# Moving each batch's norm two attention slots ahead, with temporary tiles of its own for rope

## The chip, the cores and the metric

The kernel runs on one core of one Trainium2 chip. The metric is the device time in microseconds of that core. Each time is the median of several executions.

## The reference

Four layers follow one another on an activation `x` of 4 batches, 512 positions and 512 channels, all in fp32. Only the first two matter for this change.

```python
# layer 0: modulated LayerNorm, attention with 16 heads of 32, latent keys and values, residual
h = (x - mean(x)) * rsqrt(var(x) + 1e-5) * (1 + scale) + shift
q = h @ Wq.T ; c_kv = h @ Wkd.T ; k = c_kv @ Wku.T ; v = c_kv @ Wvu.T
q, k = rope(q), rope(k)                          # z * cos + rotate_half(z) * sin
x = x + softmax(mask(q k.T / sqrt(32))) v @ Wo.T # the mask hides later blocks of 128

# layer 1: modulated RMSNorm, attention with 8 query heads of 64 and one key head, residual, gated MLP
h = x * rsqrt(mean(x * x) + 1e-6) * w * (1 + scale)
q, k = rope(h @ Wq.T), rope(h @ Wk.T) ; v = h @ Wv.T
x = x + softmax(q k.T / sqrt(64)) v @ Wo.T
x = x + (silu(h2 @ Wg.T) * (h2 @ Wu.T)) @ Wd.T
```

Layer 2 is another attention and MLP, layer 3 is a set of experts with an output projection.

## The kernel before

Activations are kept channel by position: `x` lies in SBUF as 128 partitions, 4 channel tiles, 4 batches, 512 positions. Every engine runs its own instruction stream; each engine has one semaphore that counts its finished steps, and a step waits until the count of another engine has come far enough. An instruction that waits holds everything behind it on its engine.

The attentions and all that surrounds them in layers 0 and 1 are one woven step, `layers01`. `weave` writes the order of all engines by hand. The attention of one batch of one layer is a **slot**; there are eight, `heads0` of batches 0 to 3 and then `heads1` of batches 0 to 3. A slot is a row of **quads**, four units (128 queries of one head) each: 16 quads in a slot of `heads0`, 8 in one of `heads1`. For each quad TensorE (PE) multiplies the scores (line 675), VectorE (DVE) takes the maximum (L740 with the mask, L744 without), ScalarE (ACT) the exponential (L765), PE turns the probabilities (L682), ACT and DVE copy them (L770, L747) in turns, PE multiplies by the values (L695) and spreads the reciprocal of the sums (L704), and DVE divides (L755). A unit's keys are 128 to 512 wide in layer 0, and 512 in layer 1.

A quad has four **points** at which other work, the **side** work of the slot, is inserted into every engine's stream. The side work is a list of beats; `weave` spreads the list of a slot evenly over its points. Its parts are

- the norm of a batch (`SideNorm`). For layer 0 it has seven beats: POOL sums the four tiles of x (L351, L358), an empty beat, PE takes the mean (L342) with DVE's subtraction (L394) and ACT's squares (L371), POOL sums the squares (L354, L358), an empty beat, PE takes the variance (L342) with ACT's logarithm and exponential (L376, L379, a table load before each), and last DVE scales (L406) and ACT shifts (L382). For layer 1 it has five beats, without the mean, the subtraction and the shift. The result goes to the tile `hN`, the sums to `t1`.
- the projections (`SideLinear`, L441): ten groups in layer 0, of which five read `hN` with four 512 wide products each; six groups in layer 1, all of which read `hN`.
- rope (`SideRope`): eight or five tiles. PE permutes (L474), DVE multiplies by sine into `hN[:, g % 2]` (L482), POOL multiplies by cosine (L490) and adds (L494).
- the output projection of an attention and its residual (`post`, L441 and L1314), four beats.

Before, the side work of slot m is: the norm of batch m+1 (counted over both layers), its projections, and then the output projection of slot m-1 and the rope of m+1 in turns. The norm, projection and rope of the first batch stand ahead of slot 0. In slot 0 the norm's seven beats lie in quads 0 to 4 and the first projection in quad 4; in slots 1 and 2 the norm's lie in quads 0 to 3 and the first projection follows at quad 4. In slots 3 to 6 the layer-1 norm is in quads 0 to 3 (slot 3) and 0 to 1 (slots 4 to 6), and the first projection in quad 4 and quad 2. All side matmuls inside the slots share one PSUM bank, 7, so each waits until the one before it has been read. Scores use banks 0 to 3.

Since rope writes into `hN`, the norm of the next batch waits for the last rope addition of this one (`h_free`).

SyncE (SP) issues loads in its own order. Once the last rope addition of layer 0 is done it refills the cosine and sine tables with eight transfers, and behind them it loads layer 1's query weights into the place of layer 0's (`l_wq1`), which groups 1 to 4 of `proj1` wait for. Group 0 of `proj1` uses other weights, that were loaded at the start.

Of the kernel before, what the change touches and what calls it, by code (L numbers as in the profile page):

```python
# [266 lines left out]
class Woven(Step):  # L267

    def __init__(s, seq):
# [7 lines left out]
    def waiter(s, k, e, at):  # L279
        past = dict.fromkeys(NAMES, 0)  # L280

        def after(name, b, kind, index):
            who, n = s.i[(name, b, kind, index)]
            if n > past[who]:
                past[who] = n
                e.wait_ge(k.done[who], at[who] + n)
        return after

    def pe(s, k, e, b, at):
        start_wait(k, e, at, "act", "dve", "pool")  # L290
        after = s.waiter(k, e, at)
# [3 lines left out]
    def act(s, k, e, b, at):  # L295
        start_wait(k, e, at, "act", "dve", "pe", "pool")
        after = s.waiter(k, e, at)
# [3 lines left out]
    def dve(s, k, e, b, at):  # L301
        start_wait(k, e, at, "act", "dve", "pe", "pool")
        after = s.waiter(k, e, at)
# [3 lines left out]
    def pool(s, k, e, b, at):  # L307
        start_wait(k, e, at, "act", "dve", "pe", "pool")
        after = s.waiter(k, e, at)
# [4 lines left out]
class SideNorm:  # L314
# [24 lines left out]
    def pe(s, k, e, b, kind, i, after):  # L339
        bank = s.tab.claim(s, b, kind, i, after)  # L340
        after(s.name, b, "xsum" if kind == "mean" else "vsum", 2)
        e.matmul(bank, k.ones[:], k.t1[:, 0, :], start=True, stop=True).then_inc(k.done["pe"], 1)  # L342

    def pool(s, k, e, b, kind, i, after):
        if kind == "xsum" and i < 2:
            for c in (2 * i, 2 * i + 1):
                for key in s.x_ready(b, c):
                    after(*key)
            for key in s.t_free(b):
                after(*key)  # L350
            ins = e.tensor_tensor(k.t1[:, i, :], s.x(b, 2 * i), s.x(b, 2 * i + 1), ALU.add)  # L351
        elif kind == "vsum" and i < 2:
            after(s.name, b, "square", 2 * i + 1)
            ins = e.tensor_tensor(k.t1[:, 2 * i, :], k.t1[:, 2 * i, :], k.t1[:, 2 * i + 1, :], ALU.add)  # L354
        else:
            after(s.name, b, kind, 1)
# [4 lines left out]
    def act(s, k, e, b, kind, c, after):  # L361
        if kind == "square":
            if s.rms:
                for key in s.x_ready(b, c) + s.t_free(b):
                    after(*key)
                src = s.x(b, c)
            else:
                after(s.name, b, "mean", 0)
                after(s.name, b, "centre", c)
                src = s.h(b, c)  # L370
            ins = e.activation(k.t1[:, c, :], src, ACT.Square)  # L371
        elif kind == "log":
            after(s.name, b, "var", 0)
            for key in s.t_free(b):
                after(*key)
            ins = e.activation(k.sd, s.tab.at[(s.name, b, "var", 0)], ACT.Sqrt if s.root else ACT.Ln, bias=s.eps, scale=1.0)  # L376
        elif kind == "inverse":
            after(s.name, b, "log", 0)
            ins = e.activation(k.rstd, k.sd, ACT.Exp, scale=-0.5)  # L379
        elif kind == "shift":  # L380
            after(s.name, b, "scale", c)
            ins = e.activation(s.h(b, c), s.h(b, c), s.func, bias=s.Bias(b, c), scale=1.0)  # L382
        else:
            after(s.name, b, "xsum", 1)
            after(s.name, b, "centre", c)
# [3 lines left out]
    def dve(s, k, e, b, kind, c, after):  # L389
        if kind == "centre":  # L390
            after(s.name, b, "mean", 0)
            for key in s.h_free(b):
                after(*key)
            ins = e.tensor_tensor(s.h(b, c), s.x(b, c), s.tab.at[(s.name, b, "mean", 0)], ALU.subtract)  # L394
        elif kind == "inverse":
            after(s.name, b, "log", 0)
            ins = e.reciprocal(k.rstd, k.sd)
        else:
            after(s.name, b, "inverse", 0)
            if s.rms:  # L400
                for key in s.h_free(b):
                    after(*key)
            else:
                after(s.name, b, "square", c)
# [16 lines left out]
class SideLinear:  # L421
# [11 lines left out]
    def pe(s, k, e, b, kind, g, after):  # L433
        group = s.groups[g]
        bank = s.tab.claim(s, b, kind, g, after)
        if group.load and b == 0:
            e.wait_ge(*group.load)
        for columns, lhsT, rhs, start, stop, needs in group.mats(b):
            for key in needs:
                after(*key)  # L440
# [3 lines left out]
    def put_waits(s, b, g, after):  # L444
        after(s.name, b, "mm", g)
        for key in s.groups[g].free(b) if s.groups[g].free else ():
            after(*key)

    def act(s, k, e, b, kind, g, after):
        s.put_waits(b, g, after)  # L450
        s.groups[g].put(e, b, s.tab.at[(s.name, b, "mm", g)]).then_inc(k.done["act"], 1)

    def dve(s, k, e, b, kind, g, after):
        s.put_waits(b, g, after)
# [3 lines left out]
class SideRope:  # L458


    def __init__(s, name, tiles, ready, perm, loaded=None):
        s.name, s.tiles, s.ready, s.perm, s.loaded = name, tiles, ready, perm, loaded
# [8 lines left out]
    def pe(s, k, e, b, kind, g, after):  # L471
        bank = s.tab.claim(s, b, kind, g, after)
        after(*s.ready(b, g))
# [1280 lines left out]
```

## Time and profile before

| | |
|---|---|
| median of 3 runs | 2855.88 us (2855.48 to 2857.81) |
| the profiled execution's own time | 2853.02 us |
| its span, first to last instruction | 2851.0 us |
| mean granted TensorE clock | 0.943 |
| PE busy | 2561.1 us, 90% of the span |
| the woven step of layers 0 and 1 | from 90.6 us to about 1003 us of the span |

The span is cut into stretches below. The granted clock is given as a share of 2.4 GHz: 1.00 is the upper level and 0.50 the lower, 1.2 GHz; a number between is a mean over a stretch that holds both.

### The profile page before, as it was taken

What the parts mean: (1) busy time and instruction counts of PE and PEld (TensorE: products, weight loads), DVE (VectorE), ACT (ScalarE), POOL (GpSimd) and SP (SyncE); (2) the same over time, 40 slices, a digit from 0 to 9 for tenths busy, and PEclk for the clock granted to TensorE, in tenths of its full rate; (3) what the DMA queues carried; (4) which work ended last, traced back from release to release, by engine and by line L of the source; (5) the groups of instructions that cost most, each with busy time, mean ns of one, the idle gap of its engine ahead of it and who ended that gap; (6) DMA issues with size and microseconds to landing.
All of it is one profiled execution on the core that took longest, in us unless ns stands there. A gap on an engine that the chain in (4) does not pass through costs nothing.

```text
span 2851.0 us, 32766 instructions
## 1 busy us (share of the span) xinstructions
PE 2561.1 (90%) x13072; PEld 1549.5 (54%) x13072; DVE 1257.6 (44%) x2490; ACT 1133.4 (40%) x2422; POOL 263.4 (9%) x233
## 2 busy tenths in 40 slices
PE   5678989999999949999999789999999849999998
PEld 1244444545545518888888444444444418888733
DVE  1146455444344453434433144636356464444334
ACT  0256466544343331111111255747556352222263
POOL 2223123012011000000000110101000000000021
PEclk8879999999999979999999889999989979999999
DMA  8000000000000010000100200000000101000001
GB/s 298 27 1 1 1 1 23 1 8 8 1 8 1 1 44 23 23 23 23 37 9 0 80 0 1 1 1 1 1 1 1 42 19 44 15 30 1 0 15 44
DMA packets 35687, 61.24 MB, mean 21 GB/s; under 512 B 5184, under 2 KB 18032, under 8 KB 35024
## 3 DMA queue, kind: packets, MB, share of 16 engines
q1 hardware_dynamic: 31984, 47.20, 5.0%
q0 software_dynamic: 3552, 11.96, 1.1%
q8 instruction: 103, 1.69, 0.2%
q14 instruction: 48, 0.39, 0.0%
HBM read 52.86 MB, written 4.19 MB: 20 GB/s over the span
## 4 chain that ended last, share of the span: by engine, by line
PE 53%; DVE 5%; ACT 5%; issue 0%; POOL 0%; DVEq 0%; ACTq 0%; POOLq 0%
PE banks L970 18%; PE banks L983 12%; PE banks L441 10%; PE banks L682 3%; PE banks L675 2%; PE banks L695 2%; PE banks L527 1%; DVE sb_Pr L740 1%; DVE sb_PT L747 1%; PE banks L81 1%; PE banks L598 1%; ACT sb_Pr L765 1%; PE banks L591 1%; PE banks L87 1%; ACT sb_experts L609 1%; DVE sb_Pb L99 0%
## 5 line engine op out<-in xcount | busy, mean ns | idle before, releaser
L970 PE MATMUL banks<-sb_H,sb_Ws 128*128 128x512 f32 x2304 | 536.9, 391 | 31.1 <-DVE sb_Ws L1021 30.9
L970 PEld LDWEIGHTS banks<-sb_H,sb_Ws 128*128 128x128 f32 x2304 | 435.2, 189 | 123.8 <-issue 32.5
L765 ACT ACTIVATE sb_Pr<-sb_Pr,sb_nmax 128x512 f32<-128x512 f32 (+3 forms) x512 | 326.0, 638 | 117.4 <-DVE sb_nmax L740 115.2
L682 PEld LDWEIGHTS banks<-sb_ident,sb_Pr 128*128 128x128 f32 x2176 | 251.6, 147 | 210.4 <-issue 90.0
L682 PE MATMUL banks<-sb_ident,sb_Pr 128*128 128x128 f32 x2176 | 327.5, 292 | 28.2 <-ACT sb_PT L770 21.9
L675 PE MATMUL banks<-sb_R 32*128 32x512 f32 (+4 forms) x1280 | 305.9, 602 | 45.1 <-DVE sb_nmax L740 30.3
L747 DVE COPY sb_PT<-banks 128x512 f32<-128x512 f32 (+3 forms) x320 | 195.3, 610 | 333.4 <-PE banks L682 330.8
L740 DVE CUSTOM_DVE_ANT_0 sb_Pr<-banks,sb_bias 128x512 f32<-128x512 f32 (+3 forms) x512 | 290.9, 581 | 92.9 <-PE banks L675 91.9
L983 PE MATMUL banks<-sb_hidH,sb_Ws 128*128 128x512 f32 x1024 | 325.2, 389 | 0.0
L770 ACT ACTIVATE sb_PT<-banks 128x512 f32<-128x512 f32 (+3 forms) x320 | 169.2, 529 | 349.5 <-PE banks L682 348.8
L441 PE MATMUL banks<-sb_hN,sb_W 128*128 128x512 f32 x576 | 273.3, 622 | 12.3 <-ACT sb_hN L382 9.6
L675 PEld LDWEIGHTS banks<-sb_R 32*128 32x128 f32 (+1 forms) x1280 | 105.3, 192 | 200.4 <-issue 80.8
L983 PEld LDWEIGHTS banks<-sb_hidH,sb_Ws 128*128 128x128 f32 x1024 | 192.1, 188 | 39.8
L983 PE MATMUL banks<-sb_hidL,sb_Ws 128*128 128x512 f32 x512 | 199.2, 389 | 0.0
L441 PEld LDWEIGHTS banks<-sb_hN,sb_W 128*128 128x128 f32 x576 | 110.7, 201 | 138.1 <-issue 125.1
L1035 DVE TENSOR_TENSOR sb_hidL<-sb_hN,sb_hidH 128x512 fp32r<-128x512 f32 x128 | 88.6, 692 | 205.8 <-ACT sb_hidH L1004 205.8
L441 PE MATMUL banks<-sb_A,sb_W 128*128 128x512 f32 x384 | 174.6, 600 | 3.4 <-DVE sb_hN L482 3.4
L695 PE MATMUL banks<-sb_PT,sb_V 128*32 128x256 f32 (+2 forms) x2304 | 169.7, 381 | 1.8 <-DVE sb_rsum L751 0.9
L1004 ACT ACTIVATE sb_hidH<-sb_hN 128x512 fp32r<-128x512 f32 x128 | 80.9, 632 | 186.3 <-DVE sb_hN L1029 184.2
L1029 DVE TENSOR_TENSOR sb_hN<-sb_t,banks 128x512 f32<-128x512 f32 x64 | 44.0, 687 | 247.9 <-PE banks L970 195.5
L998 ACT ACTIVATE sb_hN<-banks,sb_cols 128x512 f32<-128x512 f32 x64 | 44.0, 688 | 248.4 <-PE banks L970 248.4
L996 ACT ACTIVATE sb_t<-banks 128x512 f32<-128x512 f32 x64 | 38.3, 599 | 245.7 <-PE banks L970 245.7
(172 smaller groups left out, 2575.4 us busy)
## 6 DMA issues: line engine op xcount, KB each, us to landing
sb_WM<-in_L_cond_Wfc SPq DMA_DIRECT2D x16, 512.0 KB, 4.2
sb_WM<-in_L_cond_Wada SPq DMA_DIRECT2D x6, 1024.0 KB, 5.1
sb_x<-in_x SPq DMA_DIRECT2D x4, 1024.0 KB, 13.6
sb_WM<-in_L_cond_Wg SPq DMA_DIRECT2D x8, 512.0 KB, 3.4
sb_WM<-in_L_cond_Wu SPq DMA_DIRECT2D x8, 512.0 KB, 4.4
sb_WM<-in_L_cond_Wd SPq DMA_DIRECT2D x8, 512.0 KB, 3.6
out_x<-sb_x SPq DMA_DIRECT2D x4, 1024.0 KB, 4.5
sb_W<-in_L_cond_Wqkv POOLq DMA_DIRECT2D x1, 3072.0 KB, 10.5
```

The lines of the kernel that those rows point to most:

```text
L441: mm = e.matmul(bank[:, columns], lhsT, rhs, start=start, stop=stop)
L675: mm = e.matmul(k.bank(n % 4)[:, 0:s.width(u)], s.q(b, c)[rows, i * P:(i + 1) * P], s.k(b, c)[rows, 0:s.width(u)], start=True, stop=True)
L682: mm = e.transpose(bank[:, j * P:(j + 1) * P], k.Pr[:, n % 6, j * P:(j + 1) * P], k.ident[:])
L695: mm = e.matmul(bank[rows, 2 * P * ip + skip:2 * P * (ip + 1)], s.v(b, j, s.vhead(c, hl)), s.PT[:, n % 2, hl, j, skip:2 * P], start=j == 0 ...
L740: ins = e.tensor_tensor_reduce(k.Pr[:, n % 6, 0:s.width(u)], S, k.bias[:, s.units[u][2], 0:s.width(u)], -1.0, 3.0e38, ALU.add, ALU.min, s. ...
L747: ins = e.tensor_copy(*s.turned(k, b, u))
L765: ins = e.activation(prob, prob if s.biased else k.bank(n % 4)[:, 0:s.width(u)], ACT.Exp, bias=s.stat(k, k.nmax, b, u), scale=-1.0 if s.bi ...
L770: ins = e.activation(*s.turned(k, b, u), ACT.Copy)
L970: mm = e.matmul(k.bank(s.ups * t + w), lhsT, rhs, start=i == 0, stop=i == len(mats) - 1)
L983: mm = e.matmul(k.bank(4 + m), lhsT, rhs, start=i == 0, stop=i == len(mats) - 1)
L1004: ins = e.activation(k.hidH[:, st % 2, t, :], k.hN[:, 2 * (st % 2) + t, :], ACT.Copy)
L1035: ins = e.tensor_tensor(k.hidL[:, st % 2, t, :], k.hN[:, 2 * (st % 2) + t, :], k.hidH[:, st % 2, t, :].bitcast(F32), ALU.subtract)
```

## The change

The side work of slot m becomes: the projections of batch m+1 first (`lead`), and then three lists merged evenly by their places: the output projection of slot m-1, the rope of m+1, and the norm of batch **m+2**. So the norm for the projections of a slot has been done in the slot before. The norms of batches 0 and 1 of layer 0 both stand ahead of slot 0. Rope gets two temporary tiles, `ropet`, and doesn't write into `hN` any more; the norm then waits for the last product that reads `hN` (`proj0 mm 5`, and the last one of `proj1`) in place of the last rope addition, and the rope of a batch waits for the last rope addition of the batch before. The squares of the norm share `t1` with the latent keys; that wait (`proj0 mm 9`) stays.

```diff
@@ SideRope
-    def __init__(s, name, tiles, ready, perm, loaded=None):
+    def __init__(s, name, tiles, ready, perm, tmp_free, loaded=None):
...
-        e.tensor_tensor(k.hN[:, g % 2, :], s.tab.at[(s.name, b, "perm", g)], k.sinr[:], ALU.mult)
+        e.tensor_tensor(k.ropet[:, g % 2, :], s.tab.at[(s.name, b, "perm", g)], k.sinr[:], ALU.mult)
...
-            ins = e.tensor_tensor(z, z, k.hN[:, g % 2, :], ALU.add)
+            ins = e.tensor_tensor(z, z, k.ropet[:, g % 2, :], ALU.add)
@@ tiles
+                k.ropet = over(inner, "ropet", [P, 2, T])
@@ norm0, norm1: h_free
-                         lambda b: [("rope0", b - 1, "add", 7)] if b else [],
+                         lambda b: [("proj0", b - 1, "mm", 5)] if b else [],
...
-                         lambda b: [("rope1", b - 1, "add", 4)] if b else [("rope0", B - 1, "add", 7)],
+                         lambda b: [("proj1", b - 1, "mm", 5) if b else ("proj0", B - 1, "mm", 5)],
@@ the lists
-        sides = [beats(*[(stage, 0) for stage in pre0])]
+        def among(*parts):
+            placed = [((2 * i + 1) / (2 * len(part)), n, ops) for n, part in enumerate(parts)
+                      for i, ops in enumerate(part)]
+            return [ops for _, _, ops in sorted(placed, key=lambda entry: entry[:2])]
+        def pre(m, *which):
+            stages, b = pres[m] if m < 2 * B else ((), 0)
+            return beats(*[(stages[i], b) for i in which if stages])
+        sides = [pre(0, 0, 1, 2) + pre(1, 0)]
         for m in range(2 * B):
-            side, last, late = [[]] * 8, [], beats(posts[m - 1]) if m else []
-            if m + 1 < 2 * B:
-                (norm, proj, rope), b = pres[m + 1]
-                side, last = beats((norm, b), (proj, b)), beats((rope, b))
-            side += [ops for i in range(max(len(late), len(last))) for part in (late, last) for ops in part[i:i + 1]]
-            sides.append(side + [[]])
+            late = beats(posts[m - 1]) if m else []
+            lead = pre(m + 1, 1) or [[]] * 8
+            sides.append(lead + among(late, pre(m + 1, 2), pre(m + 2, 0)) + [[]])
```

The rest of the diff rewrites how waits are issued: the helper `after` returns the waits, and each place issues them on its engine, in the order in which they stood.

## Rows read from the trace of the kernel before

**Rows 1.** The page: busy time of PE, and its granted clock in 40 slices of the span.

```profile
PE 2561.1 (90%) x13072; PEld 1549.5 (54%) x13072; DVE 1257.6 (44%) x2490; ACT 1133.4 (40%) x2422; POOL 263.4 (9%) x233
PEclk8879999999999979999999889999989979999999
```

**Rows 2.** Windows: start:end, length, busy time (instructions) of each engine, granted clock, DMA.

```profile
150.00:180.00 30.00, 21.08 (x89) 11.28 (x90) 14.28 (x50) 18.70 (x52) 12.54 (x11) 0.56 0.00 0
...
225.00:250.00 25.00, 23.84 (x199) 12.68 (x197) 18.35 (x56) 16.07 (x48) 18.57 (x15) 1.00 0.00 1
...
250.00:285.00 35.00, 27.79 (x183) 16.32 (x182) 19.37 (x62) 25.25 (x65) 9.03 (x8) 0.80 0.00 1
285.00:365.00 80.00, 76.50 (x516) 39.23 (x515) 39.35 (x125) 39.36 (x116) 17.12 (x14) 0.98 0.00 1
365.00:400.00 35.00, 27.17 (x199) 15.81 (x198) 21.21 (x65) 26.48 (x67) 10.79 (x9) 0.81 0.00 1
...
485.00:515.00 30.00, 23.13 (x172) 13.31 (x171) 15.19 (x51) 20.40 (x55) 3.78 (x3) 0.89 0.17 53
...
595.00:625.00 30.00, 24.72 (x130) 12.55 (x128) 11.58 (x19) 16.93 (x35) 3.75 (x3) 0.77 0.04 11
...
705.00:725.00 20.00, 16.82 (x72) 9.02 (x71) 9.75 (x16) 13.38 (x28) 3.76 (x3) 0.83 0.03 8
...
810.00:830.00 20.00, 16.89 (x68) 8.77 (x70) 8.67 (x15) 11.46 (x25) 1.80 (x2) 0.83 0.00 0
```

**Rows 3.** Timeline, head of slot 1: start, length, what, [idle before <-releaser].

```profile
262.38 1.53 PE L675 MATMUL banks<-sb_R 32*128 32x384 f32 x4 [1.85 <-DVE sb_nmax L740]
...
269.95 1.28 ACT L376 ACT_TABLE_LOAD   x1
...
271.25 0.69 ACT L376 ACTIVATE sb_Pb<-banks,sb_eps 128x512 f32<-128x512 f32 x1
...
273.25 0.63 ACT L379 ACTIVATE sb_Pb<-sb_Pb 128x512 f32<-128x512 f32 x1
...
274.40 1.51 PE L682 MATMUL banks<-sb_ident,sb_Pr 128*128 128x128 f32 x6 [2.44 <-ACT sb_PT L770]
```

**Rows 4.** Timeline, the two norms of layer 0 around the start of slot 0.

```profile
90.56 2.47 POOL L351 TENSOR_TENSOR sb_t<-sb_x 128x512 f32<-128x512 f32 x2 [68.22 <-DVE sb_comb L1294]
...
107.39 2.74 DVE L406 SCALAR_TENSOR_TENSOR sb_hN<-sb_hN,sb_mod,sb_Pb 128x512 f32<-128x512 f32 x4 [8.21 <-ACT sb_Pb L379]
...
108.18 2.71 ACT L382 ACTIVATE sb_hN<-sb_hN,sb_mod 128x512 f32<-128x512 f32 x4 [0.82 <-DVE sb_hN L406]
...
109.04 19.58 PE L441 MATMUL banks<-sb_hN,sb_W 128*128 128x512 f32 x40 [4.35 <-ACT sb_hN L382]
...
114.93 0.60 ACT L1306 ACTIVATE sb_t<-banks 128x512 f32<-128x512 f32 x1 [4.05 <-PE banks L441]
...
151.13 1.85 PE L675 MATMUL banks<-sb_R 32*128 32x256 f32 x8 [9.51 <-DVE sb_nmax L740]
...
155.30 2.48 POOL L351 TENSOR_TENSOR sb_t<-sb_x 128x512 f32<-128x512 f32 x2
...
180.72 4.09 PE L441 MATMUL banks<-sb_hN,sb_W 128*128 128x512 f32 x8
...
184.85 0.60 ACT L1306 ACTIVATE sb_t<-banks 128x512 f32<-128x512 f32 x1 [1.09 <-PE banks L441]
```

**Rows 5.** Timeline at the head of slot 3, with SP's issue of layer 1's query weights.

```profile
482.84 1.27 POOL L494 TENSOR_TENSOR sb_R<-sb_R,sb_hN 128x512 f32<-128x512 f32 x1
...
487.05 0.71 PE L675 MATMUL banks<-sb_R 32*128 32x256 f32 x6
...
489.31 0.59 SPq L1592 DMA_DIRECT2D sb_W<-in_L_cond_Wq  x1
```

**Rows 6.** DMA issues by line: count, KB each, median us from issue to landing.

```profile
sb_W<-in_L_cond_Wq SPq DMA_DIRECT2D x1, 1024.0 KB, 5.9
```

More of the change, by code:

```diff
@@ L339, in pe @@
     def pe(s, k, e, b, kind, i, after):
-        bank = s.tab.claim(s, b, kind, i, after)
-        after(s.name, b, "xsum" if kind == "mean" else "vsum", 2)
+        bank = s.tab.claim(e, s, b, kind, i, after)
+        for due in after(s.name, b, "xsum" if kind == "mean" else "vsum", 2):
+            e.wait_ge(*due)
         e.matmul(bank, k.ones[:], k.t1[:, 0, :], start=True, stop=True).then_inc(k.done["pe"], 1)
@@ L434, in pe @@
         group = s.groups[g]
-        bank = s.tab.claim(s, b, kind, g, after)
+        bank = s.tab.claim(e, s, b, kind, g, after)
         if group.load and b == 0:
@@ L486, in pool @@
         if kind == "cos":
-            after(s.name, b, "perm", g)
+            for due in after(s.name, b, "perm", g):
+                e.wait_ge(*due)
             if s.loaded and g == 0:
@@ L516, in pe @@
         if kind == "sum":
-            bank = s.tab.claim(s, b, kind, i, after)
+            bank = s.tab.claim(e, s, b, kind, i, after)
             for c in range(C):
-                after(s.name, b, "square", (i, c))
+                for due in after(s.name, b, "square", (i, c)):
+                    e.wait_ge(*due)
             for c in range(C):
@@ L523, in pe @@
             w, c = i
-            bank = s.tab.claim(s, b, kind, i, after)
-            after(s.name, b, "inverse", 0)
+            bank = s.tab.claim(e, s, b, kind, i, after)
+            for due in after(s.name, b, "inverse", 0):
+                e.wait_ge(*due)
             rows = slice(32 * c, 32 * c + 32)
@@ L546, in dve @@
         if kind == "guard":
-            after(s.name, b, "sum", 1)
+            for due in after(s.name, b, "sum", 1):
+                e.wait_ge(*due)
             ins = e.tensor_scalar(k.sd, s.tab.at[(s.name, b, "sum", 1)], 1e-24, None, ALU.max)
@@ L584, in pe @@
     def pe(s, k, e, b, kind, index, after):
-        bank = s.tab.claim(s, b, kind, index, after)
+        bank = s.tab.claim(e, s, b, kind, index, after)
         if b == 0:
@@ L604, in act @@
             q, t, h = index
-            after(s.name, b, "up", index)
+            for due in after(s.name, b, "up", index):
+                e.wait_ge(*due)
             if q >= 2 or b >= 1:
-                after(s.name, b if q >= 2 else b - 1, "down", (q - 2) % C)
+                for due in after(s.name, b if q >= 2 else b - 1, "down", (q - 2) % C):
+                    e.wait_ge(*due)
             tile = 2 * (2 * q + h) + t
@@ L677, in pe @@
         elif kind == "turn":
-            after(s.name, b, "exp", u)
-            bank = s.tab.claim(s, b, kind, u, after)
+            for due in after(s.name, b, "exp", u):
+                e.wait_ge(*due)
+            bank = s.tab.claim(e, s, b, kind, u, after)
             n = s.first[b] + u
@@ L698, in pe @@
         else:
-            after(s.name, b, "recip", u)
-            bank = s.tab.claim(s, b, kind, u, after)
+            for due in after(s.name, b, "recip", u):
+                e.wait_ge(*due)
+            bank = s.tab.claim(e, s, b, kind, u, after)
             for i in range(TT):
@@ L759, in act @@
         if kind == "exp":
-            after(s.name, b, "max", u)
+            for due in after(s.name, b, "max", u):
+                e.wait_ge(*due)
             n = s.first[b] + u
```

215 lines of the change are left out of this document (136 added, 79 removed).

## Prediction

> **What bounds the kernel now.** I read the page first: PE is busy for 90% of the span, and its granted clock is high except in single slices [rows 1]. So over the whole kernel PE is the bound, and a change that moves work of ACT, DVE and POOL can only win where PE is idle or slow. Then I cut layers 0 and 1 into windows [rows 2]. For each I take the loss, which is the window's length less PE's busy time times the granted clock: it counts idle time and the half-rate time together. This treats all PE work as if it shrank with the clock, which is roughly so.
>
> From 225 to 250 us, where attention runs with little but rope beside it, the loss is 25 − 23.84 = 1.2 us. From 285 to 365 us, with projections, rope and output projection beside it, it is 80 − 76.50 × 0.98 = 5.0 us. The six heads of slots 1 to 6 are another matter:
>
> - slot 1, 250 to 285: 35 − 27.79 × 0.80 = 12.8
> - slot 2, 365 to 400: 35 − 27.17 × 0.81 = 13.0
> - slot 3, 485 to 515: 30 − 23.13 × 0.89 = 9.4
> - slot 4, 595 to 625: 30 − 24.72 × 0.77 = 11.0
> - slot 5, 705 to 725: 20 − 16.82 × 0.83 = 6.0
> - slot 6, 810 to 830: 20 − 16.89 × 0.83 = 6.0
>
> Together 58.2 us. These are the places where the norm lies, and where no projection, rope or output projection stands in PE's order. The timeline of slot 1's head shows how it comes about [rows 3]. DVE's four subtractions of the norm hold back the maxima, and PE waits 1.85 us for a score bank. Then ACT spends from 269.95 to 273.88, 3.93 us, on two table loads, the logarithm and the exponential; the copy of turned probabilities stands behind these, and PE waits 2.44 us for it. Around such waits the granted clock falls, so the next products cost double. The head of slot 0 (150 to 180) loses 30 − 21.08 × 0.56 = 18.2 us, but the change treats that one in another way.
>
> **What the change does, part by part.** The number of instructions stays: as many norms, projections and rope tiles. Only their places change.
>
> *The norm leaves the heads of slots 1 to 6.* Projections now begin at the first point of each slot, so PE has 3.4 us groups there. In the timeline of the first projections 40 such products run without a gap in 19.58 us, the first of them at the lower clock [rows 4]; with two of these groups per quad of layer 0 PE is denser than ACT and DVE, as it is now from 285 on. I take all 58.2 us of head loss away at first: −58.2.
>
> *The norm's new place takes some of it back.* Six norms (batches 2 and 3 of layer 0, four of layer 1) now lie in the second part of slots 0 to 5. A layer-0 norm brings the two waits of rows 3, 1.85 + 2.44 = 4.3 us, if nothing covers them. What may cover them is a rope product (under 1 us) or an output projection (3.4 us) at the neighbouring points. In slot 0 there is no output projection, and ACT and DVE are about as full as PE once the norm is among them: I add 3 us for clock and queueing. So slot 0 costs 7.3 and slot 1 4.3. The layer-1 norm has no subtraction; in slots 2 and 3, among layer-0 units, it costs the 2.44 us wait and some clock, 3 us each. In slots 4 and 5 an output projection stands right behind the logarithm in PE's order and covers most of it: 1 us each. Sum +19.6. The bounds: nearly nothing, if the neighbours cover all (6 us, about one wait in half the places), and 40 us, two thirds of what the heads lose now, if each wait again draws the clock down. I choose 20, nearer to the waits themselves than to the waits with their clock, since projections and output projections fill PE in the same slots.
>
> *The second norm ahead of slot 0.* It was woven into the first five quads; now PE, DVE and ACT reach the first unit behind it. POOL sets its start: rope's additions end at 155.3, as before, and the sums start there [rows 4]. The first norm shows how long the chain is: from 90.56 to the end of DVE's scaling (107.39 + 2.74) 19.6 us, and to the end of ACT's shifts 20.3 us. So DVE's first maximum moves from about 151 to 174.9, some 24 us. But PE is the bound, and what counts is its work. By 180.72, where the projections of batch 1 begin now, PE has done 21.08 × 0.56 = 11.8 us of work since 150, of which the norm's mean and variance are some 1.7, and 0.5 us of scores before 150: 10.6 us of attention that the new order still has to do. In return the new order begins those projections when the first shift is done: the chain puts this at 155.3 + (109.04 − 90.56) = 173.8 by the same distance. A first group from the lower clock takes 114.93 − 109.04 = 5.9 us, so it ends at 179.7, where it ends at 184.8 now: 5.1 us won. Cost 10.6 − 5.1 = 5.5, and a half more because the first two groups now follow one another on the one side bank, and the second waits for the copy of the first: +6. The bounds are 4 and, if the delay of the maxima counts in full, 24.
>
> *The query weights of layer 1.* They are loaded behind the last rope addition of layer 0, and nothing in the change moves that. It ends at 484.1; SP issues eight table transfers first and the weights at 489.31 [rows 5]; they land 5.9 us later [rows 6], at 495.2. At present their first reader comes in quad 4, long after. Now group 1 of `proj1` stands at the first point of quad 1. PE reaches quad 1's scores at 487.05 [rows 5]; group 0 in front of it adds 3.4, and the scores and the first turned units some 1.5: 492. PE waits 3 us, with all of attention behind it: +3, between 0 and 6.
>
> *At nothing:* the tiles `ropet` (same instructions, other addresses, and POOL's additions keep their two buffers); the wait of the norm for `proj mm 5`, which comes quads earlier; the wait for `proj0 mm 9`, whose product stands before POOL's sums in the same slot; the table refill for the next rope, which has a whole slot's head as cover (it is a matter of some 7 us from the last addition, against two quads with five groups); and the rewritten waits, which are the same ones. Without their cover each costs a few us at most.
>
> A rule of the Trainium skill weighs against the norm's new place. The rows show a table load of 1.28 us with the logarithm right behind it (269.95 + 1.28 = 271.23, start at 271.25), so that the pair holds ACT for 3.93 us [rows 3]. The page "ScalarE: Activation LUTs", section "What ACT_TABLE_LOAD costs", gives about 1.28 us for the load and about 1.38 us more for a drain, 2.66 us for each switch. By it, as an estimate, ACT would be held 2.8 us longer for each norm, and the six would give back some 17 us more; the trace doesn't show that drain here, and the sum goes by the trace.
>
> **The sum.** −58.2 + 19.6 + 6 + 3 = −29.6 us against the profiled execution, 2853.0, which gives 2823.4. The median of the runs shown is 2.9 above that execution, so the forecast is 2826 us.
>
> **The rivals.**
>
> *A: only half comes back.* PE's waits and the fallen clock travel with the norm: each of the six pays about 6.7 us, 40 in all. For it speaks that at 225 to 250 us DVE is busy 18.35 and ACT 16.07 of 25 even without a norm, so there is little slack; against it, that the 80 us from 285 hold everything else and lose only 5. −58.2 + 40 + 9 = −9: 2847 us. Chance 0.2.
>
> *B: more comes back.* The side products cover the waits, the weights arrive in time, and some of the loss within slots goes too: −58.2 + 6 + 4 = −48: 2808 us. For it, the layer-1 slots, where ACT has much slack; against it, slot 0. Chance 0.15.
>
> *C: slower.* The chain of attention through DVE and ACT, not PE, sets the pace of the slots. Then the 24 us by which the first maximum comes later count in full, and a denser PE in the heads wins little, because ACT's and DVE's norm work only changes its place. It decides once what the heads give back, net, falls under 24 + 3 = 27 us; at 20 us it gives +7, 2863 us. For it, PE waits for maxima and exponentials wherever it waits at all; against it, PE's 95% and more outside the heads [rows 2]. Chance 0.05.
>
> *D: the change changes nothing that counts,* since the norm's loss is the same wherever it lies and the start costs little: within 0.2%. Chance 0.03.
>
> The clock is the soft spot of all of them: the rows show it at the lower level in stretches with a few microseconds of idle PE. The page "TensorE: Matmul & The Clock Gate", section "What's actually happening", says that the throttled state is the default and activity releases it; the granted clock of the six heads agrees, and it is the way by which A could come about.
>
> **How the numbers follow.** The forecast has 0.57, with a range of its own from 2816 to 2837 us. The range that is to hold 8 in 10 reaches from B to near A: 2808 to 2846 us. A difference of 0.2%, 5.7 us, is about what can be told from no change here. Faster by more: forecast, B and most of A, 0.91. Within it: 0.04. Slower by more: 0.05.
>
> **What would show it.** In the windows of the changed kernel the heads of slots 1 to 6 should lose under 2 us each, with the clock near 1.00. DVE's first maximum should come near 175 us, and the first wide product of batch 1's projections just before it. PE should wait once, some 3 us, for the query weights at the head of slot 3, and 2 to 3 us for ACT's copy behind each variance. The end of the woven step should come 30 us earlier, with all after it unchanged. The prediction is wrong if slot 0 becomes much longer than 85 us from its first maximum, if waits for `nmax` grow in the second halves, or if the clock is low there.

## The result

The changed kernel takes 2843.36 us (median of 6 runs, 2839.03 to 2846.87) against 2855.68 us (2853.25 to 2857.81) for the kernel before. The ratio is 0.9958, with a 95% interval of 0.9945 to 0.9970. It is faster by 12.3 us. The forecast was 29.6 us, so less than half of it came. The time lies inside the range given for 8 in 10, outside the forecast's own range (2816 to 2837), and 3.6 us from rival A.

The profiled execution of the changed kernel took 2841.46 us (span 2839.4), 11.6 us less than that of before. The page, to set beside [rows 1]:

```profile
PE 2549.7 (90%) x13072; PEld 1539.6 (54%) x13072; DVE 1260.0 (44%) x2490; ACT 1135.2 (40%) x2422; POOL 263.9 (9%) x233
...
PEclk8879999999999979999999889999989979999999
```

As many instructions as before; PE is busy 11.4 us less, and its mean granted clock is 0.949 in place of 0.943. Lines after the helper's change are numbered anew: scores L725, turns L733, values L749, projections L464, maxima L799 and L803, exponentials L828, copies L806 and L833, the norm's scaling L428, shift L396, table loads in L388 and L392, rope's addition L525.

Windows of the changed kernel, columns as in [rows 2]: first slot 0 from DVE's first maximum to its last rope sine, then the heads of slots 1 to 6, with the lengths that they had in before:

```profile
176.00:272.40 96.40, 86.83 (x578) 44.23 (x580) 52.86 (x179) 62.40 (x176) 25.26 (x20) 0.92 0.00 1
272.00:307.00 35.00, 33.20 (x219) 17.18 (x219) 13.23 (x45) 16.36 (x47) 2.55 (x2) 0.99 0.00 1
380.00:415.00 35.00, 33.34 (x208) 17.60 (x208) 14.19 (x49) 18.64 (x53) 1.71 (x2) 1.00 0.00 1
487.00:517.00 30.00, 26.96 (x157) 13.45 (x159) 10.44 (x40) 14.60 (x44) 1.50 (x2) 0.94 0.17 53
590.00:620.00 30.00, 28.26 (x173) 13.91 (x172) 15.78 (x35) 15.18 (x38) 2.55 (x2) 1.00 0.07 18
689.00:709.00 20.00, 17.57 (x90) 9.72 (x90) 10.17 (x17) 6.88 (x17) 2.81 (x2) 0.83 0.11 27
792.00:812.00 20.00, 17.57 (x90) 10.14 (x89) 10.30 (x16) 6.93 (x16) 2.82 (x2) 0.83 0.11 27
```

By the prediction's measure (length less busy time times clock) the heads of slots 1 to 6 lose 2.1, 1.7, 4.7, 1.7, 5.4 and 5.4 us, 21 in place of 58. The heads of slots 5 and 6 still run at 0.83, and no table load lies in them. Their timeline does. The layer-1 norm's last beat, four scalings, comes just after the last rope sine, so it falls into the first microseconds of the next slot:

```profile
689.65 0.68 DVE L510 TENSOR_TENSOR sb_ropet<-banks,sb_sin 128x512 f32<-128x512 f32 x1
...
690.35 3.83 DVE L428 SCALAR_TENSOR_TENSOR sb_hN<-sb_x,sb_comb,sb_Pb 128x512 f32<-128x512 f32 x4
690.77 1.54 POOL L525 TENSOR_TENSOR sb_R<-sb_R,sb_ropet 128x512 f32<-128x512 f32 x1
...
692.10 1.13 PE L725 MATMUL banks<-sb_R 64*128 64x512 f32 x4
694.11 0.68 DVE L803 TENSOR_REDUCE sb_nmax<-banks 128x1 f32<-128x512 f32 x1
...
694.82 0.69 ACT L828 ACTIVATE sb_Pr<-banks,sb_nmax 128x512 f32<-128x512 f32 x1 [2.46 <-DVE sb_nmax L803]
...
695.65 3.27 PE L725 MATMUL banks<-sb_R 64*128 64x512 f32 x4 [2.42 <-ACT sb_Pr L828]
```

Read it as a chain: DVE scales for 3.83 us; the maximum that stands behind comes at 694.11; ACT waited 2.46 us for it; PE waited 2.42 us for ACT to free a score bank. Then four score products take 3.27 us, where four took 1.13 us just before. The granted clock, 1.00 up to the wait, is 0.52 from 695.60 to 699.00, the lower level, and ACT frees the banks one by one.

Slot lengths say where the forecast and the kernel part. A slot ends where its last rope sine starts, and the whole is cut without gaps from 0; profiled executions, in us:

| | up to the end of slot 0 | slot 1 | 2 | 3 | 4 | 5 | 6 | all that follows |
|---|---|---|---|---|---|---|---|---|
| before | 249.2 | 117.0 | 115.4 | 107.2 | 107.7 | 102.8 | 102.6 | |
| after | 272.4 | 108.1 | 106.8 | 103.3 | 99.1 | 102.6 | 99.4 | |
| measured | +23.2 | −8.9 | −8.6 | −3.9 | −8.6 | −0.2 | −3.2 | −1.3 |
| forecast | +13.3 | −8.5 | −10.0 | −3.4 | −10.0 | −5.0 | −6.0 | 0 |

The last row sorts the prediction's own terms by slot (the start's 6 and slot 0's 7.3; slot 1's −12.8 + 4.3; and so on), and adds up to −29.6. Slots 1 to 3 came near the forecast, within 1.4 us each. The miss of 18 us is 10 in slot 0 and 9 in slots 4 to 6.

### The profile page after: what moved, and what is told of

Same layout as the page of the kernel before. It is cut to its first block, busy times and chain, and to the rows that moved or that the text cites. A ratio compares the mean times of both kernels' runs of the same rounds, so it can differ in the third digit from the quotient of the medians.

```text
span 2839.4 us, 32777 instructions
## 1 busy us (share of the span) xinstructions
PE 2549.7 (90%) x13072; PEld 1539.6 (54%) x13072; DVE 1260.0 (44%) x2490; ACT 1135.2 (40%) x2422; POOL 263.9 (9%) x233
## 4 chain that ended last, share of the span: by engine, by line
PE 53%; DVE 5%; ACT 5%; issue 0%; POOL 0%; DVEq 0%; ACTq 0%; POOLq 0%
PE banks L1036 18%; PE banks L1049 12%; PE banks L464 10%; PE banks L733 4%; PE banks L725 3%; PE banks L749 2%; PE banks L560 1%; DVE sb_Pr L799 1%; DVE sb_PT L806 1%; PE banks L81 1%; PE banks L639 1%; PE banks L631 1%; PE banks L87 1%; ACT sb_experts L652 1%; ACT sb_Pr L828 0%; DVE sb_Pb L99 0%
## 5 line engine op out<-in xcount | busy, mean ns | idle before, releaser
L828 ACT ACTIVATE sb_Pr<-sb_Pr,sb_nmax 128x512 f32<-128x512 f32 (+3 forms) x512 | 326.6, 639 | 100.6 <-DVE sb_nmax L799 98.5
L733 PEld LDWEIGHTS banks<-sb_ident,sb_Pr 128*128 128x128 f32 x2176 | 244.6, 144 | 201.7 <-issue 87.4
L733 PE MATMUL banks<-sb_ident,sb_Pr 128*128 128x128 f32 x2176 | 319.3, 286 | 23.1 <-ACT sb_PT L833 14.4
L799 DVE CUSTOM_DVE_ANT_0 sb_Pr<-banks,sb_bias 128x512 f32<-128x512 f32 (+3 forms) x512 | 291.6, 582 | 100.3 <-PE banks L725 99.2
L806 DVE COPY sb_PT<-banks 128x512 f32<-128x512 f32 (+3 forms) x320 | 195.3, 610 | 313.7 <-PE banks L733 309.8
L725 PE MATMUL banks<-sb_R 32*128 32x512 f32 (+4 forms) x1280 | 302.3, 590 | 24.2 <-DVE sb_nmax L799 15.6
L833 ACT ACTIVATE sb_PT<-banks 128x512 f32<-128x512 f32 (+3 forms) x320 | 169.4, 529 | 327.3 <-PE banks L733 326.4
L464 PE MATMUL banks<-sb_hN,sb_W 128*128 128x512 f32 x576 | 272.9, 621 | 19.2 <-ACT sb_hN L396 13.2
L1049 PEld LDWEIGHTS banks<-sb_hidH,sb_Ws 128*128 128x128 f32 x1024 | 192.3, 188 | 39.7
L725 PEld LDWEIGHTS banks<-sb_R 32*128 32x128 f32 (+1 forms) x1280 | 103.7, 188 | 181.4 <-issue 83.8
L464 PEld LDWEIGHTS banks<-sb_hN,sb_W 128*128 128x128 f32 x576 | 109.5, 199 | 148.6 <-issue 125.5
L464 PE MATMUL banks<-sb_A,sb_W 128*128 128x512 f32 x384 | 174.9, 601 | 0.0
L749 PE MATMUL banks<-sb_PT,sb_V 128*32 128x256 f32 (+2 forms) x2304 | 167.9, 377 | 1.8 <-DVE sb_rsum L811 0.9
```

The costliest lines, as they stand in the source:

```text
L464: mm = e.matmul(bank[:, columns], lhsT, rhs, start=start, stop=stop)
L725: mm = e.matmul(k.bank(n % 4)[:, 0:s.width(u)], s.q(b, c)[rows, i * P:(i + 1) * P], s.k(b, c)[rows, 0:s.width(u)], start=True, stop=True)
L733: mm = e.transpose(bank[:, j * P:(j + 1) * P], k.Pr[:, n % 6, j * P:(j + 1) * P], k.ident[:])
L749: mm = e.matmul(bank[rows, 2 * P * ip + skip:2 * P * (ip + 1)], s.v(b, j, s.vhead(c, hl)), s.PT[:, n % 2, hl, j, skip:2 * P], start=j == 0 ...
L799: ins = e.tensor_tensor_reduce(k.Pr[:, n % 6, 0:s.width(u)], S, k.bias[:, s.units[u][2], 0:s.width(u)], -1.0, 3.0e38, ALU.add, ALU.min, s. ...
L806: ins = e.tensor_copy(*s.turned(k, b, u))
```

## The experiments

Each time is the median of 4 to 11 executions, its ratio is to the kernel before in the same session, with the 95% interval. "Changed kernel" is the one with the change, 2843.4 us. Where two of the changed versions are compared, their ranges tell how firmly. Slot lengths come from one profiled execution each; slot 2, with the same side work, takes 106.8 us in the changed kernel and 109.1 with the start undone, so 2 us in one layer-0 slot tell nothing.

### The start by itself, and its undoing

Old order everywhere, but the norm of batch 1 ahead of slot 0, in rope's own tiles:

```diff
-        sides = [pre(0, 0, 1, 2)]
+        sides = [pre(0, 0, 1, 2) + pre(1, 0)]
...
-            side = pre(m + 1, 0, 1) or [[]] * 8
+            side = (pre(m + 1, 0, 1) if m else pre(1, 1)) or [[]] * 8
```

> Only one part of the change: the norm of batch 1 of layer 0 stands ahead of slot 0, its projections and rope follow in slot 0; all other norms stay at the heads of their slots as in the kernel before, and rope has its own tiles. Theory S (the start costs what the forecast said, 6 us): about 2862 us, slot 0 some 6 us longer than before. Theory T (the start costs 13 to 16 us, since the attention work that slot 0 did around the norm at the lower clock was worth about 17 us and not 10.6, the small transposes not getting shorter with the clock in proportion): about 2870 us, and the last rope sine of slot 0 some 13 us or more later than before, with the slots 1 to 6 as long as before.

Measured: 2861.35 us (2859.14 to 2862.89), ratio 1.0022 [1.0014, 1.0031], slower by 6.3 us. The start costs what the forecast said, 6, and the theory that asked 13 to 16 of it falls.

```diff
-        sides = [pre(0, 0, 1, 2) + pre(1, 0)]
+        sides = [pre(0, 0, 1, 2)]
...
-            lead = pre(m + 1, 1) or [[]] * 8
+            lead = (pre(m + 1, 1) if m else pre(1, 0, 1)) or [[]] * 8
```

> The changed kernel, but the norm of batch 1 is woven into slot 0 ahead of its projections, as before; all other norms two slots ahead. Theory S: 6 us less than the changed kernel, about 2837. Theory T: 12 to 16 us less, 2828 to 2831. Rival: the gain is smaller, 0 to 4 us, because slot 0 now holds two norms and the second is squeezed.

Measured, on the changed kernel: 2835.03 us (2831.89 to 2839.77), 0.9933 [0.9921, 0.9945]: 8.3 us less than the changed kernel. Alone it cost 6.3, with the rest of the change 8.3; the ranges of the runs are as wide as this difference.

### The norms of the last two batches back at their heads

```diff
-            lead = pre(m + 1, 1) or [[]] * 8
-            sides.append(lead + among(late, pre(m + 1, 2), pre(m + 2, 0)) + [[]])
+            lead = (pre(m + 1, 0, 1) if m in (5, 6) else pre(m + 1, 1)) or [[]] * 8
+            ahead = pre(m + 2, 0) if m < 4 else []
+            sides.append(lead + among(late, pre(m + 1, 2), ahead) + [[]])
```

> The changed kernel, but the norms of batches 2 and 3 of layer 1 stand at the heads of slots 5 and 6, ahead of their projections, as before. Theory S (a norm in slots 4 and 5 costs 1 us each in its new place and 6 at the head): 10 us slower than the changed kernel, 2853. Theory M (in its new place it costs as much as at the head, since the four scalings hold DVE and with it the maxima): within 2 us of the changed kernel, 2843.

Measured: 2840.45 us (2839.31 to 2844.84), 0.9954 [0.9942, 0.9966], not slower than the changed kernel. Slots 4 to 6 take 96.2, 102.4 and 102.4 us, 301.0 together, against 99.1, 102.6 and 99.4, 301.1. Slot 4, which now holds nothing of a norm but the last beat of the one before, is 11.5 us shorter than before: the forecast's 11.0 for its head was right. But moving the norms of slots 5 and 6 wins nothing: together they cost in their new places what they cost at the heads. The forecast had said 1 for 6, twice.

Slot 4 of this run has a second use. It has the burst of four near its start, uncut as in the changed kernel, and still takes only 96.2 us:

```profile
595.18 2.74 DVE L428 SCALAR_TENSOR_TENSOR sb_hN<-sb_x,sb_comb,sb_Pb 128x512 f32<-128x512 f32 x4
```

### The scaling spread out

The four scalings (and in layer 0 their shifts) one to a beat, in both layers' norms. The cut shows layer 1's:

```diff
+        if s.rms and s.fine:
+            return [squares] + tail + [[op] for op in scales]
         if s.rms:
             return [squares] + tail + [scales]
...
```

> The changed kernel, but the four scalings of a norm (and the four shifts in layer 0) stand in four beats, one tile in each, instead of one beat. Theory S (the scalings cost next to nothing in the new place): 0 to 2 us faster than the changed kernel. Theory M (the burst of scalings makes PE wait 1.6 to 2.4 us in each of slots 0, 4 and 5 and draws the clock down behind it): 6 to 12 us faster, 2831 to 2837, with no wait of PE for the maxima or exponentials over 1 us at the ends of slots 0, 4 and 5 and the clock at 1.00 there.

Measured: 2837.06 us (2836.63 to 2842.34), 0.9944 [0.993, 0.9958], 6.3 less than the changed kernel. Three more beats also shift the places of all the others, and a new wait appears:

```profile
660.15 1.02 PE L351 MATMUL banks<-sb_t,sb_ones 128*128 128x512 f32 x2
...
663.76 0.69 ACT L394 ACTIVATE sb_Pb<-banks,sb_eps 128x512 f32<-128x512 f32 x1
...
664.50 2.08 PE L506 MATMUL banks<-sb_R,sb_perm 128*128 128x512 f32 x2 [3.33 <-ACT sb_Pb L394]
```

Behind the variance (660.15) PE's next side product is a rope tile (664.50). It needs the one side bank, which ACT's logarithm reads last; PE waits 3.33 us. In the changed kernel turns of PE and then the output projection stood there.

Then with two beats of two in layer 1, and four of one in layer 0 as in the last:

```diff
-            return [squares] + tail + [[op] for op in scales]
+            return [squares] + tail + [scales[:2], scales[2:]]
```

> The changed kernel, with the scalings and shifts of a layer-0 norm in four beats of one tile, and the scalings of a layer-1 norm in two beats of two tiles. In e4 the four scaling beats pushed the variance of a layer-1 norm right ahead of a rope product, which waited 3.3 us for the one side bank until the logarithm had read it; with pairs an output projection stands there instead, one point later. Theory M (the burst of scalings was the cost in slots 4 and 5, the bank wait what e4 put in its place): 3 to 7 us less than e4, 2830 to 2834. Theory S (the scalings cost nothing): as e4 or as the changed kernel, 2837 to 2843.

Measured: 2829.99 us (2826.13 to 2834.26), 0.9912 [0.9898, 0.9925], 13.4 less than the changed kernel.

The pairs in layer 1 by themselves, layer 0's norm as changed:

> The changed kernel, with one edit: the four scalings of a layer-1 norm (batches 0 to 3, in slots 2 to 5) come in two beats of two instead of one beat of four. Layer 0's norms are as changed. Same work, same number of instructions. Theory M (the burst of four scalings on VectorE, not ScalarE's logarithm and exponential, is what the norm costs in the layer-1 slots): slots 4 to 6 shrink as they did when both layers' norms were split, where they came down from 301 to 288 us together; what slots 2 and 3 lose again is at most 9 us. So 4 to 13 us less than the changed kernel, 2830 to 2839, with the clock of slots 4 and 5 near 1.00. Forecast's theory (only ScalarE's pair and the subtraction cost anything; the burst costs nothing): no difference from the changed kernel, 2843, within 3 us.

Measured: 2828.17 us (2827.81 to 2828.91), 0.9905 [0.9891, 0.9918], 15.2 less than the changed kernel. The windows of slots 4, 5 and 6, first of the changed kernel, then of this one:

```profile
590.50:689.70 99.20, 95.85 (x555) 50.80 (x556) 45.46 (x84) 46.41 (x106) 16.79 (x14) 1.00 0.02 6
689.70:792.30 102.60, 97.87 (x502) 52.21 (x500) 43.51 (x72) 43.60 (x97) 16.63 (x14) 0.97 0.02 6
792.30:891.70 99.40, 96.22 (x515) 52.95 (x512) 44.06 (x73) 39.26 (x92) 12.69 (x10) 0.97 0.02 6
```

```profile
591.50:687.20 95.70, 93.63 (x553) 50.49 (x554) 46.45 (x84) 46.33 (x106) 16.73 (x14) 1.00 0.03 6
687.20:783.40 96.20, 93.46 (x502) 50.46 (x500) 44.41 (x71) 43.66 (x97) 16.62 (x14) 1.00 0.03 6
783.40:879.20 95.80, 93.63 (x516) 51.04 (x512) 42.72 (x70) 39.20 (x92) 12.72 (x10) 1.00 0.03 6
```

DVE and ACT do the same work; PE's clock is 1.00 throughout, and the three slots take 287.7 in place of 301.2 us, 13.5 less. The theory that expected no difference falls.

Not all of the 13.5 is shown to be the burst's, for one more beat in the list shifts the places of the others too. The heads of slots 5 and 6, where the chain above was read, lose 1.8 and 1.4 us here in place of 5.4 and 5.4:

```profile
686.50:706.50 20.00, 18.17 (x97) 9.27 (x96) 10.15 (x16) 9.09 (x22) 2.82 (x2) 1.00 0.11 27
783.10:803.10 20.00, 18.58 (x100) 9.68 (x102) 9.81 (x15) 8.60 (x20) 2.82 (x2) 1.00 0.11 27
```

That is 7.6 us. Slot 6 shows it cleanest: it holds a burst and nothing else of a norm, its own beats stay where they were, and it is 3.6 us shorter with the burst in pairs. The other 6 us came in slot 4 (3.5) and in the rest of slot 5. In slot 4 of the changed kernel the clock is 1.00, and no wait of PE is longer than 0.8 us; without a norm in its second part, but with the burst at its start, it took 96.2 us in the run above. So most of slot 4's excess hangs on the other beats of the norm, and these have moved. In the changed kernel a rope product comes right behind an output projection and waits for the side bank, and the variance is taken 10 us before the slot ends:

```profile
672.79 1.13 PE L500 MATMUL banks<-sb_R,sb_perm 128*128 128x512 f32 x2 [0.78 <-DVE sb_x L1381]
...
679.86 1.12 PE L345 MATMUL banks<-sb_t,sb_ones 128*128 128x512 f32 x2
```

With the pairs the variance is taken 22 us before the slot ends, and the side products stand farther apart:

```profile
665.41 1.12 PE L348 MATMUL banks<-sb_t,sb_ones 128*128 128x512 f32 x2
```

No run moves the beats without cutting the burst, so which of the moved beats cost what stays open.

The split of layer 0's norm, which the run before this one had besides the pairs, wins nothing overall: by it slot 0 (from the last rope sine ahead of it) falls from 121.6 to 112.1 us, and slots 1 to 3 together rise from 320.4 to 331.4.

### No table switch

The logarithm of these norms replaced by a second exponential, so that ACT stays in one table. This changes the factor of the normalisation; the number of operations stays.

```diff
-            ins = e.activation(k.sd, s.tab.at[(s.name, b, "var", 0)], ACT.Sqrt if s.root else ACT.Ln, bias=s.eps, scale=1.0)
+            ins = e.activation(k.sd, s.tab.at[(s.name, b, "var", 0)], ACT.Sqrt if s.root else ACT.Exp if s.name in ("norm0", "norm1") else ACT.Ln, bias=s.eps, scale=0.001 if s.name in ("norm0", "norm1") else 1.0)
```

> The changed kernel, with the logarithm in the norms of layers 0 and 1 replaced by a second exponential of a small multiple, so that ScalarE never leaves the exponential's table there: the two table loads of each norm (1.28 us each) are gone, and the factor of the normalisation is no longer the right one. Everything else is as changed. Forecast's theory (ScalarE's pair is what holds up TensorE, once uncovered in slots 0 to 3 and covered in 4 and 5): the six norms inside slots 0 to 5 give back 2.44 us in each of slots 0 to 3 and little in 4 and 5, and the norms of batches 0 and 1 ahead of slot 0 are 2.6 us shorter each: 10 to 15 us less, 2828 to 2833. Theory M (the burst of scalings holds up TensorE): slots 4 and 5 keep their lengths of 99.1 and 102.6 us within 1 us; slots 0 to 3 give back at most 1 us each, and the start at most 5: 2 to 9 us less, 2834 to 2841.

Measured: 2838.82 us (2836.4 to 2841.68), 0.9942 [0.9929, 0.9956], 4.5 less than the changed kernel, with ranges that overlap; slots 4 and 5 keep 99.1 and 102.4 us. The first maximum comes at 171.2 in place of 176.0 us, slot 0 from there is 2.1 us shorter, and slots 1 to 3 together are not shorter (320.8 for 318.2 us). So the loads cost something at the start, perhaps something in slot 0, and nothing in slots 4 and 5. The theory that ACT's pair is what holds PE up asked for 10 to 15 us and falls, as far as the loads go: they are 2.6 of the pair's 3.9 us, and the two operations stay. The burst and its wait are there as before:

```profile
676.81 0.69 ACT L388 ACTIVATE sb_Pb<-banks,sb_eps 128x512 f32<-128x512 f32 x1 [2.03 <-PE banks L345]
677.53 0.63 ACT L392 ACTIVATE sb_Pb<-sb_Pb 128x512 f32<-128x512 f32 x1
...
686.14 3.83 DVE L428 SCALAR_TENSOR_TENSOR sb_hN<-sb_x,sb_comb,sb_Pb 128x512 f32<-128x512 f32 x4
...
690.60 0.69 ACT L828 ACTIVATE sb_Pr<-banks,sb_nmax 128x512 f32<-128x512 f32 x1 [2.46 <-DVE sb_nmax L803]
...
691.43 3.27 PE L725 MATMUL banks<-sb_R 64*128 64x512 f32 x4 [2.42 <-ACT sb_Pr L828]
```

### Slot 0's second norm

Changed kernel, but the norm of batch 2 at the head of slot 1, so that slot 0 holds none:

```diff
-            lead = pre(m + 1, 1) or [[]] * 8
-            sides.append(lead + among(late, pre(m + 1, 2), pre(m + 2, 0)) + [[]])
+            lead = (pre(m + 1, 0, 1) if m == 1 else pre(m + 1, 1)) or [[]] * 8
+            ahead = pre(m + 2, 0) if m else []
+            sides.append(lead + among(late, pre(m + 1, 2), ahead) + [[]])
```

> The changed kernel, but the norm of batch 2 of layer 0 stands at the head of slot 1, ahead of its projections, as before, and not in slot 0; slot 1 so holds two norms, slot 0 none. Theory S (7.3 us in slot 0, 12.8 at the head): 5 us slower than the changed kernel, 2848. Theory P (in slot 0, where nothing of PE's covers it, a norm costs 14 to 16 us, as much as at the head): within 3 us of the changed kernel, or up to 3 us faster, with slot 0 some 15 us shorter and slot 1 some 13 longer.

Measured: 2839.38 us (2838.77 to 2843.11), 0.9948 [0.9935, 0.996], 4.0 less than the changed kernel, with ranges that overlap. From the first maximum to its end slot 0 takes 80.4 us without a norm, and 96.4 with one. The window of the run with the start alone, which also has none there, agrees:

```profile
176.30:257.00 80.70, 76.40 (x559) 40.11 (x560) 46.50 (x166) 51.24 (x158) 17.88 (x15) 0.97 0.00 1
```

So a norm in the second part of slot 0 costs some 16 us. At slot 1's head it makes slot 1 12.4 us longer, and slot 2 is 3.3 longer too, so it isn't shown that it costs less there. The changed kernel's slot 0 shows the same pattern as slot 5, four scalings and a late maximum:

```profile
263.04 2.73 DVE L428 SCALAR_TENSOR_TENSOR sb_hN<-sb_hN,sb_mod,sb_Pb 128x512 f32<-128x512 f32 x4
...
265.68 0.55 DVE L799 CUSTOM_DVE_ANT_0 sb_Pr<-banks,sb_bias 128x384 f32<-128x384 f32 x1
...
266.30 2.88 PE L725 MATMUL banks<-sb_R 32*128 32x512 f32 x4 [1.63 <-DVE sb_nmax L799]
```

The 20 us from 255 lose 20 − 15.62 × 0.83 = 7.0 us:

```profile
255.00:275.00 20.00, 15.62 (x128) 7.58 (x120) 11.55 (x31) 14.68 (x34) 5.56 (x5) 0.83 0.00 0
```

### The tiles alone

The old order, with `ropet` and the new waits:

```diff
-        e.tensor_tensor(k.hN[:, g % 2, :], ...)
+        e.tensor_tensor(k.ropet[:, g % 2, :], ...)
```

> The kernel before in its old order, with rope's own temporary tiles and the new waits of the norm. All theories: the time of before within 0.2%, 2855 us. If the tiles or the rewritten waits matter (the DVE scaling meets a POOL addition more often, or the norm starts sooner), more than 3 us off.

Measured: 2856.18 us (2854.55 to 2857.53), 1.0004 [0.9995, 1.0013]: nothing, as forecast.

### Better versions

The split of both norms as in the fifth run (fine in layer 0, pairs in layer 1), and the start undone:

> As e5, and the norm of batch 1 woven into slot 0 ahead of its projections, as before. If the two costs add (e2 gave 8 us less than the changed kernel), 6 to 9 us less than e5, about 2825. If they don't, because slot 0 then holds two norms whose last beats are the ones that e5 spread, within 3 us of e5.

Measured: 2820.79 us (2815.21 to 2823.48), 0.9877 [0.9863, 0.989].

The pairs alone, and the start undone:

> The changed kernel with two edits: the norm of batch 1 is woven into slot 0 again, and the scalings of a layer-1 norm come in two beats of two. Layer 0's norms are as changed. If the two costs are separate, they add: 2843 less 8.3 for the start and less 15.2 for the pairs gives 2820, within 3 us. If the split of layer 0's norm in the run that had both (2820.8) was worth something there, this one is slower than that by 3 us or more.

Measured: 2821.34 us (2821.05 to 2824.54), 0.9878 [0.9861, 0.9894]. The costs add, and layer 0's split shows no gain here either. Last, the norm of batch 2 at slot 1's head as well:

> As the last, and the norm of batch 2 stands at the head of slot 1 too, so that the norms of the first three batches lie where they lay before and only those of batch 3 and of layer 1 stand a slot ahead, the latter with their scalings in pairs. If the price of the second norm in slot 0 is paid whatever lies beside it, and what it cost at slot 1's head is 4 us less (2839.4 against 2843.4), this gives 2816 us, within 3. If slot 0 gets its second norm cheaper once the start is undone, so that nothing is left to win, it stays at 2820.

Measured: 2817.60 us (2815.33 to 2826.14), 0.9871 [0.9852, 0.9889]. Slots 0 and 1 take 218.0 us against 222.5 in the run before it, which agrees with the 4.0 of the norm of batch 2; the times alone, whose ranges overlap, don't separate the two versions. All three beat both kernels. The last keeps from the change only the norms of batch 3 and of layer 1 a slot ahead, and is 38 us faster than before.

## Why the prediction was wrong

**The step that failed** is "The norm's new place takes some of it back", +19.6. The sign and the mechanism of the whole were right, this term was mis-sized. In it, the prediction let only the subtraction and ACT's pair hold PE up, put 1 us on the norm of each layer-1 slot, and left the last beat, the scalings, out. What came back was about 40 us, worked out from profiled executions: −11.6 measured, plus the 58.2 of the heads, less 6.3 for the start and 0.6 for the weights, is 39.7. By place, against the prediction's terms:

- *Slots 4 to 6: 11.0 us for 2.* The heads' 23.0 less the measured 12.0. The prediction priced ACT's pair here and found its cover; without table loads slots 4 and 5 are as long, so the loads aren't the cost. But the norm's last beat, the four scalings, was priced at nothing, though [rows 4] show it at 2.74 us of DVE. No maximum stood behind it in the stretch that was read; in the slots the maxima do. The bursts at the heads of slots 5 and 6 cost 7.6 us, by the chain that was read and by the pairs. The other 6 of the 13.5 us that the pairs gave lie in slot 4 and the rest of slot 5, and seem to hang on where the norm's beats stand among the side products, which no run tests by itself. In pairs nothing comes back in these slots.
- *Slot 0: 16.9 us for 7.3.* The measured 23.2 less the start's 6.3; two runs with no norm there put it at 15.7 and 16.0. That DVE and ACT are full there was named, the size was taken too small, with 3 us for clock and queueing. The sign of being wrong that the prediction gave has come: 96.4 us from the first maximum, for 85. The end of the slot, with the burst, loses 7.0 of it. The rest isn't pinned to one wait: spreading the scalings shortened slot 0 by 9 us and lengthened the next three by more, so in the layer-0 slots the burst isn't the whole cause. This stays open.
- *Slots 1 to 3: 13.2 us for 10.3.* The heads' 35.2 less the measured 21.4 and the 0.6 for the weights.
- *After the attentions* 1.3 us went, of which no experiment tells the cause.

**The heads' loss, −58.2, was right where it was tested, in slots 4 to 6.** Slot 4 without a norm is 11.5 us shorter (11.0 forecast). Slots 5 and 6, once their norms' scalings are in pairs, are 6.5 and 6.8 shorter than before (6.0 forecast for each head). For slots 1 to 3 no run separates the heads' gain from what the norms cost in their new places.

**The start, +6, was right.** 6.3 us by itself, and 8.3 when it is undone in the changed kernel. The mean's product starts at 160.51 us, the first projection at 175.00 (forecast 173.8), and takes 6.32 for 5.9; the first maximum comes at 176.0 (174.9).

**The weights, +3, were too dear.** PE waits 0.61 us for them, for 3. SP issues them at 494.50 (489.31 before), and they land 5.3 us later, but PE is late too, since group 0 ran 5.20 us at a lower clock and its copy follows:

```profile
491.14 5.20 PE L464 MATMUL banks<-sb_hN,sb_W 128*128 128x512 f32 x8
...
494.50 0.58 SPq L1668 DMA_DIRECT2D sb_W<-in_L_cond_Wq  x1
...
499.87 0.70 PE L464 MATMUL banks<-sb_hN,sb_W 128*128 128x512 f32 x1 [0.61 <-DMA sb_W<-in_L_cond_Wq]
```

**The tiles at nothing** was right.

**The rivals.** A, half comes back, is the one that happened, and almost to its number (40 us returned). Part of that is luck: it has 6.7 us for each of six norms, and slot 0 alone cost 16.9. Its reasoning held for the clock, not for the waits. At the head of slot 5 the kernel before has PE wait 2.91 us for an exponential that stands behind ACT's pair:

```profile
715.03 1.28 ACT L379 ACT_TABLE_LOAD   x1
...
718.16 2.74 PE L675 MATMUL banks<-sb_R 64*128 64x512 f32 x4 [2.91 <-ACT sb_Pr L765]
```

That wait went. In its place came the one of 2.42 us behind the scalings, in the same slot, and like the first it took the clock down with it. C asked that the delay of the first maximum count in full, and the start alone shows that it doesn't. B fell with the term above. D, no change that counts, fell too, by 12.3 us against 5.7, though the two norms of the run with slots 5 and 6 behave as it says. With the bursts of layer 1 in pairs the kernel takes 2828.2 us, near the 2826 forecast, but by luck: slot 0 is still too long, and slots 4 to 6 are shorter than forecast.

**The page on the table loads.** The prediction set the trace's 1.28 us for a load against 2.66 in the Trainium skill ("ScalarE: Activation LUTs", section "What ACT_TABLE_LOAD costs"). The run without switches shows the difference directly: from the logarithm's start to the exponential's are 677.53 − 676.81 = 0.72 us, and in the changed kernel, with a load between, 683.02 − 681.02 = 2.00 us. A load costs 1.28 us here, and no drain is seen.

```profile
681.02 0.69 ACT L388 ACTIVATE sb_Pb<-banks,sb_eps 128x512 f32<-128x512 f32 x1 [0.72 <-PE banks L345]
681.73 1.28 ACT L392 ACT_TABLE_LOAD   x1
681.76 3.70 PE L464 MATMUL banks<-sb_A,sb_W 128*128 128x512 f32 x8
...
683.02 0.63 ACT L392 ACTIVATE sb_Pb<-sb_Pb 128x512 f32<-128x512 f32 x1
```

## What to carry to other kernels

When a stage is moved, price every beat of it in the new place, on every engine, and first the longest run of instructions that has no wait inside: whoever stands behind it may wait for its whole length. Here a burst of 3.8 us on an engine that is 44% busy cost some 4 us at each of two heads, because PE's wait of 2.4 us also took its clock down. Cutting a beat in two also moves the beats around it, and that may have been worth nearly as much here (6 of 13.5 us); a cut into four put a rope product before a bank that was still being read. So read the new order after each such edit, and not only the piece that was cut.

## What was not expected of the hardware

Scalings of DVE and an addition of POOL slow one another. Four scalings in layer 1 take 2.73 us where no addition falls among them, and 3.83 where one does, as at 690.35 above, where that addition took 1.54 in place of 1.27 us. The first timeline row is of a burst alone, the other lines give the shortest, median and longest in ns, of each line's instructions in the changed kernel:

```profile
593.69 2.73 DVE L428 SCALAR_TENSOR_TENSOR sb_hN<-sb_x,sb_comb,sb_Pb 128x512 f32<-128x512 f32 x4
```

```profile
L428 DVE SCALAR_TENSOR_TENSOR sb_hN<-sb_x,sb_comb,sb_Pb x16: 736/744/1761, 482.9 to 796.1; 128x512 f32<-128x512 f32 x16
```

```profile
L525 POOL TENSOR_TENSOR sb_R<-sb_R,sb_ropet x52: 1261/1268/1537, 136.6 to 893.1; 128x512 f32<-128x512 f32 x52
```

One scaling of four takes 1.76 in place of 0.74 us, so it is held for 1.0 us, and not all four a little. The Trainium skill states such a rule ("SBUF — State Buffer", section "SBUF: two separate sides"): a VectorE operation with two SBUF inputs and a GpSimd operation that reads SBUF take the same pair of ports as an exclusive lock, and the second waits for the first. The rows agree with it. What the 1.1 us are worth in the burst's price wasn't tried by itself. The pairs don't escape it: at slot 5's head the second pair takes 2.51 us, where a pair alone takes 1.41, and PE's clock stays at 1.00 there.

```profile
687.88 2.51 DVE L431 SCALAR_TENSOR_TENSOR sb_hN<-sb_x,sb_comb,sb_Pb 128x512 f32<-128x512 f32 x2
```
